# FFN's second stage with w2's high and low parts side by side, 512 columns at once

## What is computed

```python
x = x + tanh(g_xattn[0]) * attention(layernorm(x), ctx_1024, ctx_1024)   # 16 heads, causal
xf = layernorm(x)                                     # what the FFN reads, 256 features a token
prob = softmax(xf @ w_router + b_router)              # 16 blocks, the best 4 are used
mask = top_4_of(prob)
h = relu(einsum('nd,ebd->neb', xf, w1b) + b1b)        # 1024 hidden features
y = einsum('neb,ebd,ne->nd', h, w2b, mask) + b2       # back to 256: the FFN's second stage
x = x + tanh(g_ffn[0]) * y
```

## Time and profile before

| | us |
|---|---|
| median of 3 runs | 681.58 (681.28 to 682.12) |
| the profiled execution | 680.97 |
| its span in the trace | 679.1 |
| PE busy | 659.7 (97%) |
| DVE busy | 527.8 (78%) |
| ACT busy | 538.9 (79%) |
| POOL busy | 556.0 (82%) |

### The profile page before, as it was taken

The page is one execution under the profiler, slowest core; times in us unless marked ns, Lnnn a source line. Parts: engine busy times, 40 slices in busy tenths (PEclk is TensorE's granted clock), DMA queues, the critical chain, the costliest instruction groups (busy, mean ns, idle before and its releaser), DMA issues.

```text
span 679.1 us, 30579 instructions
## 1 busy us (share of the span) xinstructions
PE 659.7 (97%) x12960; PEld 611.9 (90%) x12960; DVE 527.8 (78%) x1429; ACT 538.9 (79%) x785; POOL 556.0 (82%) x718
## 2 busy tenths in 40 slices
PE   6779999999999999999999999999999999999997
PEld 5668899999999999999999999989999999999997
DVE  6899887788777778788778878777878877877742
ACT  4668788888888888888888888888888888887732
POOL 6677888988988898888898898888888889887643
PEclk9899999999999999999999999999999999999999
DMA  5323355556545446645556654544554554553110
GB/s 197 96 55 86 88 109 99 116 109 115 120 114 116 99 110 116 111 112 113 100 117 107 116 111 122 103 107 114 113 113 112 116 100 96 98 86 64 28 40 32
DMA packets 192279, 69.24 MB, mean 102 GB/s; under 512 B 166160, under 2 KB 191888, under 8 KB 192144
## 3 DMA queue, kind: packets, MB, share of 16 engines
q1 hardware_dynamic: 191312, 65.72, 45.7%
q10 hardware_dynamic: 832, 1.57, 0.6%
HBM read 19.03 MB, written 8.39 MB: 40 GB/s over the span
## 4 chain that ended last, share of the span: by engine, by line
PE 86%; DVE 5%; DMA 3%; ACT 2%; issue 2%; POOL 1%; SPq 1%; POOLq 0%; DVEq 0%
PE bank L423 11%; PE score_banks L344 10%; PE bank L357 8%; PE score_banks L314 8%; PE bank L425 8%; PE bank L424 8%; PE bank L446 8%; PE bank L447 8%; PE bank L448 8%; PE bank L371 4%; PE bank L401 2%; PE score_banks L327 1%; DMA used_all<-used 1%; PE bank L393 1%; ACT weights L525 1%
## 5 line engine op out<-in xcount | busy, mean ns | idle before, releaser
L880 POOL TENSOR_TENSOR h_low<-hid,h_high 128x512 fp32r<-128x512 f32 x128 | 164.2, 1283 | 12.8 <-ACT hid L560 12.8
L738 DVE SCALAR_TENSOR_TENSOR hid<-bank,b_cols,used_all 128x256 f32<-128x256 f32 x248 | 108.1, 477 | 65.9 <-PE bank L425 58.2
L873 POOL TENSOR_SCALAR_AFFINE_SELECT weights<-weights 128x1024 f32<-128x1024 f32 x128 | 138.2, 1103 | 18.2 <-ACT weights L525 16.4
L423 PE MATMUL bank<-xT_high,w_high 128*128 128x256 f32 x496 | 151.5, 305 | 0.8 <-DVE hid L738 0.7
L525 ACT ACTIVATE weights<-score_banks 128x1024 f32<-128x1024 f32 x128 | 124.3, 1024 | 34.7 <-PE score_banks L344 34.6
L424 PE MATMUL bank<-xT_low,w_high 128*128 128x256 f32 x496 | 139.4, 281 | 0.0
L425 PE MATMUL bank<-xT_high,w_low 128*128 128x256 f32 x496 | 139.4, 281 | 0.0
L446 PE MATMUL bank<-w_high,h_high 128*128 128x256 f32 x488 | 137.3, 281 | 0.7 <-POOL h_low L880 0.7
L447 PE MATMUL bank<-w_low,h_high 128*128 128x256 f32 x488 | 137.7, 282 | 0.0
L448 PE MATMUL bank<-w_high,h_low 128*128 128x256 f32 x488 | 136.2, 279 | 0.0
L423 PEld LDWEIGHTS bank<-xT_high,w_high 128*128 128x128 f32 x496 | 93.3, 188 | 8.9 <-DVE hid L738 1.1
(11 more groups left out here) (105 smaller groups left out, 1411.1 us busy)
## 6 DMA issues: line engine op xcount, KB each, us to landing
x_in<-in_x SPq DMA_DIRECT2D x31, 256.0 KB, 3.1
out_y<-y_out SPq DMA_DIRECT2D x31, 256.0 KB, 2.2
c_in<-in_ctx SPq DMA_DIRECT2D x30, 256.0 KB, 2.8
qT<-qT SPq DMA_DIRECT2D x128, 4.0 KB
w_stage<-in_w1T ACTq DMA_DIRECT2D x1, 1024.0 KB, 9.2
hid<-in_w2T SPq DMA_DIRECT2D x8, 128.0 KB, 2.7
kT_parts<-k_parts SPq DMA_TRANSPOSE x57, 2.8
qT_parts<-q_parts SPq DMA_TRANSPOSE x57, 2.7
```

Source lines behind the costliest of these rows:

```text
L423: pe.matmul(out=bank, lhsT=w1_high[:, k, c], rhs=high, start=k == 0, stop=False)
L738: dve.scalar_tensor_tensor(hid[:, n % 4, j], hid_bank(n)[:, j * TOKS:(j + 1) * TOKS], b1_cols[:, c:c + 1], used_all[:, p % 2], ALU.add, AL ...
L873: pool.affine_select(out=w, in_=w, compare_op=ALU.is_ge, fill=0.0, base=0, pattern=[[0, 2 * HB], [1, S]], channel_multiplier=-1).then_inc( ...
L880: pool.tensor_tensor(h_low[:, p % 2, chunks], hid[:, n % 4], h_high[:, p % 2, chunks].bitcast(F32), ALU.subtract).then_inc(h_low_made, 1)
```

## The change

w2's two parts are kept in one tile, `w2_parts`, chunk by chunk with the 256 high columns and then the 256 low ones. For each chunk one matmul with h_high takes all 512 columns (line 446 of the changed kernel); its high half goes to columns 0 to 255 of the bank and its low half to columns 256 to 511. The second matmul, h_low with the high part (line 448), adds 256 columns into 0 to 255 as before. VectorE then adds the two halves of the bank in two steps: x2_b2 = upper half * tanh_g + x2_b2 (line 716 of the changed kernel), a wait for that write, and y_out = lower half * tanh_g + x2_b2 (line 719).

```diff
-        w2_high = sb("w2_high", [P, HC, D], F32R)
-        w2_low = sb("w2_low", [P, HC, D], F32R)
+        w2_parts = sb("w2_parts", [P, HC, 2, D], F32R)
...
-            return 1, w2_stage[:, c], w2_high[:, c], w2_low[:, c]
+            return 1, w2_stage[:, c], w2_parts[:, c, 0], w2_parts[:, c, 1]
...
-                    pe.matmul(out=bank[:, 0:D], lhsT=high, rhs=w2_high[:, c, :], start=a, stop=False)
-                    pe.matmul(out=bank[:, 0:D], lhsT=high, rhs=w2_low[:, c, :], start=False, stop=False)
-                    made = pe.matmul(out=bank[:, 0:D], lhsT=low, rhs=w2_high[:, c, :], start=False, stop=z)
+                    pe.matmul(out=bank[:, 0:2 * D], lhsT=high, rhs=w2_parts[:, c].rearrange("p l n -> p (l n)"),
+                              start=a, stop=False)
+                    made = pe.matmul(out=bank[:, 0:D], lhsT=low, rhs=w2_parts[:, c, 0], start=False, stop=z)
...
                 dve.wait_ge(x2_b2_made, b + 1)
+                dve.scalar_tensor_tensor(x2_b2[:, b % GS, :], out_bank(b)[:, D:2 * D], tanh_g[:, 1:2],
+                                         x2_b2[:, b % GS, :], ALU.mult, ALU.add).then_inc(y_half_made, 1)
+                dve.wait_ge(y_half_made, b + 1)
                 dve.scalar_tensor_tensor(y_out[:, pair % 2, b % PAIR, :], out_bank(b)[:, 0:D], tanh_g[:, 1:2],
                                          x2_b2[:, b % GS, :], ALU.mult, ALU.add).then_inc(y_made, 1)
```

More of the change, by code:

```diff
@@ L179, in build @@
         ve_made = sem("ve_made")
-        xT_low_made, hid_made, y_made = (sem(n) for n in ("xT_low_made", "hid_made", "y_made"))
+        xT_low_made, hid_made, y_made, y_half_made = (sem(n) for n in (
+            "xT_low_made", "hid_made", "y_made", "y_half_made"))
         top_found, clipped_made, clipped_found, marked_made = (sem(n) for n in (
```

## The result

The changed kernel takes 686.56 us in the median of 6 runs (684.05 to 687.67), against 681.82 for the kernel before in 6 runs of its own (680.99 to 683.5). The ratio is 1.0063, with a 95% interval of 1.0042 to 1.0083: slower by 4.7 us, where I had forecast 5.5 us less. 686.56 lies above the range.

A forecast was written before the change was run, and what follows sets the result against it. TensorE, at 86% of the span, was taken as the bound, a stream without gaps. The terms -9.2 + 2.5 + 0.7 + 0.5 = -5.5 us gave 675.5 from the profiled 680.97, 676.1 for the median; range 671.5 to 683.5.

The forecast's parts named there:

- TensorE's term: ffn_out's 512 chunks: 336 ns each instead of 354, 18 less, 9.2 us off.
- The hints in the earlier trace: TensorE's weight loads stand 0.11 us apart under 64 and 128 columns, suggesting a load takes 110 to 118 ns.
- Rival 1: In ffn_out columns are the bound: 512 cost 236 ns, TensorE gains nothing, waits remain; 683.5 us, chance 0.14.
- VectorE's added step: Adding the bank's halves costs VectorE 0.52 us an iteration, made up in its idle time ahead of L738.
- The row maxima: Row maxima to shifted scores: 1.16 us of slack, 0.57 left, costing nothing in an undisturbed iteration.
- All its outputs come 0.52 us later too ... Nothing there: GpSimd waits for mv, so its outputs come later; h_low and causal weights have over 2 us, no cost.
- Waits for qT and used_all: Late q_parts and used_all through SP's DMA queue make TensorE and L738 wait in tight tiles: 2.5 us together.
- The loop of VectorE and GpSimd: L691 meeting GpSimd's L880 keeps mv late at a 9.86 us period: 0.7 us added, gain capped at 9.7.
- The end: The last tile's two VectorE steps stand behind each other with nothing to hide them: 0.5 us added.
- Rival 4: VectorE's lateness, from mv to row maxima in qT, starts a wait every second iteration: 683 to 686, chance 0.06.

The follow-up runs named there:

- the matmul alone: The changed kernel without VectorE's added step, upper half of the bank never added: 680.08 us against 682.27 for before, ratio 0.9973.
- late keys: Kernel before with k_parts behind the first half of the causal weights on GpSimd: 689.35 us; with ACT's xT copy also ahead of kT: 683.03 us.
- the added copy: Kernel before with one useless 128x256 copy on GpSimd ahead of q_parts: 690.93 us against 682.30, ratio 1.0122.
- the step alone: Changed kernel with three 256-column matmuls again, the middle one into the bank's upper half, VectorE adding the halves: 684.78 us, ratio 1.0041.

## Why the prediction was wrong

- **TensorE's term was mis-sized.** I took 18 ns a chunk, 9.2 us, on the belief that the 118 ns were the weight load. The 512 columns took 0.234 us and not 0.218, so it is 4 ns a chunk and 2 us; the matmul alone measured 2.2. The hints in the earlier trace rows were right, a load takes 0.11 us however few columns follow, but they couldn't show that 256 columns of F32R take longer than it. They take 0.118. Two limits lay 8 ns apart and I took the nearer fit for the only one. Rival 1 had this right, at 0.14. The rule of the Trainium skill ("TensorE: Matmul & The Clock Gate", section "Back-to-back issue gap"), 2.5 ns over the columns at 2.4 GHz, by which the change saves almost nothing, came out with the better verdict, though not with its number: the trace shows 0.234 us for 512 columns where it gives 0.216. That section of the Trainium skill calls the rule the gap of a single matmul, and for a stream of loads and matmuls of 512 columns it has 131 ns. This trace doesn't show that either.
- **VectorE's added step: right**, 0.52 us, and it is made up at the end of the iteration. The row maxima stay in time in the steady iterations.
- **"All its outputs come 0.52 us later too ... Nothing there"**: the step that failed in the other direction. Of the outputs of GpSimd behind `mv` I followed q_parts to qT and used_all, and h_low and the causal weights to TensorE, but not the transposed copies through SP and ACT. The slack of kT itself is indeed long. The slack of what stands behind kT in ACT's order wasn't asked for: xT, which is needed at once in every second iteration. That is most of the 5.0 us lost in the profiled execution.
- **Waits for qT and used_all: the mechanism right.** I had 2.5 us of them. The trace shows 1.3 us of loads waiting for qT in five times, and 2.4 in six where xT goes first on ACT and TensorE isn't held up at the router. So the size was fair once the other wait is out of the way; none of it is TensorE waiting for used_all.
- **The loop of VectorE and GpSimd**: its 0.7 us didn't come. In the changed kernel L691 takes 0.54 us on the mean (0.60 before), and with TensorE's gain at 0.03 us an iteration there was nothing to cap. But the meeting of L691 and L880 is real and stays on where GpSimd itself is late: 1.03 to 1.05 us on the mean in the three kernels with late keys or the added copy.
- **The end: right in size.** From the shifted scores of the last tile to the end of the span it is 47.6 us against 47.3, and 48.2 with the step alone; I had 0.5 more.
- **Rival 1's time, 683.5, was too low** for the same reason: to its missing gain it added 1.9 us, 1.4 of waits and events and 0.5 at the end, and no wait at the router. Rival 4 had a wait of VectorE's lateness in every second iteration; it named the wrong one.

The sum as it turned out, for the profiled execution (5.7 us longer in its span): 1.8 off for the matmuls, 5.0 on for the waits at L393 and others, 0.3 at the end, and 2.1 in the first nine tiles, which I can't put down to the change.

## What to carry to other kernels

When a step makes an engine late, follow every output of every engine behind it, and at each stop ask not only who needs this output but what stands behind it in the same queue: here a copy that nobody needed soon held up one that was needed at once, and turning the two round gave back 6 us by the medians, 3.7 of them shown in the steady iterations. A saved instruction is worth what the next limit leaves of it, so before merging, look for a row in which only one of the two suspected limits varies. And an engine that is idle for an eighth of its time can still be unable to take 0.4 us more at a given place. Last, an edit that leaves an engine's code alone can still make that engine late, so look at its durations before calling it untouched.

## What the runs showed of the hardware

**F32R columns.** At a granted clock of 1.00, 256 columns of F32R take 0.117 to 0.118 us in a stream and 512 take 0.234. That is 0.457 ns a column, a tenth more than one cycle of 2.4 GHz.

**Slow landings.** The DMA of k_parts lands 2.8 us after its issue on the median, but in some iterations after over 4. For the wait shown above, the DMAs between its issue and its landing, by queue (packets, MB, share) and issue (us to landing):

```profile
q1 hardware_dynamic: 1687, 0.45, 45.7%
q8 instruction: 1, 0.02, 1.4%
...
kT_parts<-k_parts SPq DMA_TRANSPOSE x1, 4.3
```

There is one packet of 16 KB in it that fetches instructions; the page has about a hundred of these in the program, 1.1 to 1.2 us long each on the mean. Of this transfer 15 of its 16 semaphore steps came by 99.32 us, and the last at 100.89. From 100 to 600 us of the traces of before and after, 17 of these DMAs took over 3.9 us, and every one had such a packet in flight; of the 60 that landed within 3.0 us with all 16 steps in the trace, 19 had one too. The time at which the packet began tells them apart: in 15 of the 17 it began 0.96 to 2.22 us behind the issue of the transfer, in all 19 it began 2.26 us or more behind it. In the kernel before, six of its seven slow ones fell in iterations without the router, where nobody minds; in the changed kernel seven of ten fell in those with it (the eighth of those above comes ahead of 100 us). That the instruction packets make the landing late is a reading of the traces and not tested, and why the two patterns fall as they do stays open. Whether it also moves the time from one execution of the changed kernel to the next, 684 to 688, isn't known: there is one trace, and the granted clock, 1.00 in the fastest and 0.99 to 0.998 in the others, goes with these times as well.
